# Layer 1, second head: in two quarters the normalised rows are turned by VectorE and sixteen transfers

## The reference

```python
h = jnp.maximum(_layernorm(x, axis=-1), 0.0)
x = x + _L0_gnn_ref(...)            # one normalised product with adj, W, relu
h = jnp.maximum(_layernorm(x, axis=-1), 0.0)
x = x + _L1_gnn_ref(...)            # two attention heads, below
...                                 # layer 2: one attention head; layer 3: product with adj.T
```

```python
h = x_norm @ ff0_w[i].T
s_src = h @ attn_w[i, :c]
s_dst = h @ attn_w[i, c:]
e = jax.nn.leaky_relu(s_src[:, None] + s_dst[None, :])
e = jnp.where(mask, e, jnp.float32(NEG))
atten = jax.nn.softmax(e, axis=1)
att = atten @ h + x
att = _ln(att, g2, b2)
h_next = h_next + jax.nn.elu(att @ ff1_w[i].T) / K
```

## Time and profile before

| | |
|---|---|
| median of 3 runs | 1198.27 us (1197.99 to 1199.12) |
| the profiled execution | 1198.28 us |
| its span, first to last instruction | 1196.5 us |
| mean granted clock of TensorE | 1.000 |
| PE / DVE / ACT busy | 1191.9 / 936.4 / 301.6 us |
| products of stages 1, 2 and 4 in the chain (L504) | 51% |
| products of stages 0 and 3 in the chain (L488) | 37% |

### The profile page before, as it was taken

One profiled execution on the slowest core, in us unless ns is written; L12 is line 12 of the kernel. 1 busy time (PEld: TensorE's weight loads), 2 busy tenths in 40 slices (PEclk: granted clock), 3 DMA queues, 4 the chain that ended last, 5 costly groups with the idle time before them and its releaser, 6 DMA issues.

```text
span 1196.5 us, 16807 instructions
## 1 busy us (share of the span) xinstructions
PE 1191.9 (100%) x6299; PEld 823.5 (69%) x6299; DVE 936.4 (78%) x1704; ACT 301.6 (25%) x732; POOL 10.4 (1%) x21
## 2 busy tenths in 40 slices
PE   9999999999999999999999999999999999999999
PEld 9999999965444444444544547999999974444455
DVE  5548675798878788878888796798787869887886
ACT  3312122234323232422323134541212121000000
POOL 3000000000000000000000000000000000000000
PEclk9999999999999999999999999999999999999999
DMA  9888888700111102110000000022303068999930
GB/s 318 301 270 289 299 293 302 254 23 10 45 18 36 18 35 35 53 18 18 1 18 0 18 1 19 2 86 109 141 0 141 1 258 305 313 332 319 321 85 18
DMA packets 79284, 153.18 MB, mean 128 GB/s; under 512 B 35456, under 2 KB 44016, under 8 KB 79216
## 3 DMA queue, kind: packets, MB, share of 16 engines
q1 hardware_dynamic: 53264, 145.43, 34.8%
q10 hardware_dynamic: 25456, 6.30, 2.4%
q0 software_dynamic: 496, 0.55, 0.1%
HBM read 144.33 MB, written 4.24 MB: 124 GB/s over the span
## 4 chain that ended last, share of the span: by engine, by line
PE 98%; DVE 1%; ACT 0%; issue 0%; DVEq 0%
PE acc L504 51%; PE acc L488 37%; PE acc L761 4%; PE mix L570 1%; PE mix L557 1%; PE mix L542 1%; PE turn L519 1%; PE acc L769 1%; DVE ring L1323 0%; PE turn L515 0%; PE mix L628 0%; PE mix L515 0%; PE turn L638 0%; DVE U L1454 0%; PE mix L645 0%; PE turn L633 0%
## 5 line engine op out<-in xcount | busy, mean ns | idle before, releaser
L1323 DVE SCALAR_TENSOR_TENSOR ring<-G,score,mask 128x1024 f32<-128x1024 f32 x372 | 464.7, 1279 | 62.8 <-PE acc L504 33.0
L504 PE MATMUL acc<-ring,G 128*128 128x512 f32 x1000 | 436.2, 593 | 0.2 <-DVE acc L1263 0.2
L504 PEld LDWEIGHTS acc<-ring,G 128*128 128x128 f32 x1000 | 186.6, 190 | 226.9 <-issue 209.8
L488 PE MATMUL acc<-G,ring 128*128 128x129 f32 x2240 | 254.3, 275 | 0.1
L488 PEld LDWEIGHTS acc<-G,ring 128*128 128x128 f32 x2240 | 252.1, 192 | 1.4 <-issue 1.1
L488 PE MATMUL acc<-G,mask 128*128 128x129 f32 x1648 | 186.2, 275 | 0.0
L488 PEld LDWEIGHTS acc<-G,mask 128*128 128x128 f32 x1648 | 185.0, 192 | 0.0
L504 PE MATMUL acc<-mask,G 128*128 128x512 f32 x384 | 165.8, 593 | 0.0
L1597 DVE TENSOR_TENSOR ring<-ring,mask 128x1024 f32<-128x1024 f32 x120 | 146.7, 1223 | 11.4 <-DVE ring L1597 0.9
L504 PEld LDWEIGHTS acc<-mask,G 128*128 128x128 f32 x384 | 72.6, 190 | 91.0 <-issue 89.8
L1361 DVE TENSOR_SCALAR mask<-mask 128x1024 uint8<-128x1024 f32 x103 | 68.6, 688 | 38.0 <-DMA mask<-in_adj_t 37.7
(11 more groups left out here) (210 smaller groups left out, 692.6 us busy)
## 6 DMA issues: line engine op xcount, KB each, us to landing
mask<-in_adj SPq DMA_DIRECT2D x128, 512.0 KB, 5.5
mask<-in_adj_t SPq DMA_DIRECT2D x103, 512.0 KB, 4.9
ring<-in_adj_t SPq DMA_DIRECT2D x18, 512.0 KB, 4.9
G<-given_rows SPq DMA_DIRECT2D x10, 512.0 KB, 3.9
G<-in_adj_t SPq DMA_DIRECT2D x4, 512.0 KB, 5.1
inputs<-V ACTq DMA_DIRECT2D x4, 512.0 KB, 2.7
V<-inputs SPq DMA_DIRECT2D x4, 512.0 KB, 3.9
X<-in_x SPq DMA_DIRECT2D x3, 512.0 KB, 9.9
```

The costliest lines, as they stand in the source:

```text
L488: mm = pe.matmul(acc[:, b, (s % 3) * DW:(s % 3) * DW + DW], lhs[:, s * P:(s + 1) * P], g, start=(k == 0 and s % 3 == 0), stop=(k == T - 1) ...
L504: mm = pe.matmul(acc[:, c, :], g, moving[:, c * BANK:(c + 1) * BANK], start=(k == 0), stop=(k == T - 1), skip_group_check=True)
L1323: dve.scalar_tensor_tensor(slots[k % L], late_home[h] if early and k >= EARLY else rows_home[h, q], rank[h][:, k:k + 1], span(mask, (q * T ...
```

## The change

`MOVED = 2`: for the quarters 0 and 1 of the second head, PE's `turned` is left out. In their place stand DVE's `small_turns` and `move_blocks`, eight transfers on SP's queue (behind `bring_back(0)` and `bring_back(1)`) and eight on ACT's, and ACT scales V, not `turn`. Quarters 2 and 3 keep PE's transposes. The counts of `blocks_moved` and `small_turned` for the last layer move up by two, and `move_blocks` is told by an argument which buffers it works on.

The lists of `stage2` for the quarters 1 and 2 of the loop change with it. On PE, `sums_back` stays behind tile 1, the transposes (13) go, `apply` moves from 15 to 17, the two steps of the feed stay at 27 and 28. On DVE:

| step | behind tile, before | after |
|---|---|---|
| residual, rest of it | 4, 5 | 4, 5 |
| statistics, half and rest | 8, 10 | 7, 8 |
| scales | 12 | 9 |
| small turns | - | 12 |
| own pattern, rest of it | 13, 16 | 14, 17 |
| elu, add | 19, 20 | 20, 21 |
| feed: half, rest, scales, halves | 21, 23, 25, 29 | 22, 23, 25, 29 |

```diff
--- before.py
+++ after.py
@@ -83,6 +83,7 @@
     EDGE = (2, 3, 0, 1)
     EB = len(EDGE)
     SPARE = 2
+    MOVED = 2
     WEIGHTS = 15
     WARM = 7
 
@@ -264,10 +265,10 @@
 
         flat_v = V[:, :, :].rearrange("p s d -> p (s d)")
 
-        def move_blocks(eng, q, groups):
+        def move_blocks(eng, q, groups, rows=True):
 
             eng.wait_ge(small_turned, q + 1)
-            given, taker = (U[:, 0:QC], flat_v) if q < Q else (part_turned, U[:, 0:QC])
+            given, taker = (U[:, 0:QC], flat_v) if rows else (part_turned, U[:, 0:QC])
             for i in groups:
                 for d in range(4):
                     src = given[32 * i:32 * i + 32, :].rearrange("p (s d r) -> p s d r", d=4, r=32)[:, :, d, :]
@@ -435,7 +436,9 @@
             move_blocks(sp, 3, (0, 1))
             sp.wait_ge(saved, 16 * Q)
             bring_back(0)
+            move_blocks(sp, Q, (0, 1))
             bring_back(1)
+            move_blocks(sp, Q + 1, (0, 1))
             bring_back(2)
             bring_back(3)
 
@@ -570,7 +573,7 @@
                         mm = pe.matmul(mixed[:, s * P:(s + 1) * P], U[:, s * P:(s + 1) * P], ff1T[:, h, :],
                                        start=True, stop=True, skip_group_check=True)
                     mm.then_inc(ff_done, 1)
-                return (sums_back, apply) if h == 0 else (sums_back, turned, apply)
+                return (sums_back, apply) if h == 0 or not fixed(q) or q < MOVED else (sums_back, turned, apply)
 
             def spread_top(i):
                 pe.wait_ge(top_placed, i)
@@ -712,7 +715,7 @@
                     ks = [1, 11, 12, 25, 26, 27, 29]
                     run(2, q, at(ks, steps + (lambda: spread_top(early_top[3]), lambda: spread_rows(m))))
                 else:
-                    ks = [1, 13, 15, 27, 28]
+                    ks = [1, 17, 27, 28]
                     run(2, q, at(ks, steps))
             stage2(0)
             pe.wait_ge(qv2_placed, 1)
@@ -1003,15 +1006,15 @@
                     settle()
                 normalise(of_v, lambda s: U3[:, s, 0:D], local(scale), local(shift), ACT.Identity, n_norm)
                 act.wait_ge(n_norm, j + 1)
-                if h == 0:
-                    move_blocks(act, q, (2, 3))
-                    act.wait_ge(blocks_moved, 256 * (q + 1))
+                if h == 0 or not fixed(q) or q < MOVED:
+                    move_blocks(act, j, (2, 3))
+                    act.wait_ge(blocks_moved, 256 * (j + 1))
                     for c in range(2):
                         half = slice(c * BANK, (c + 1) * BANK)
                         ins = act.activation(U[:, half], flat_v[:, half], ACT.Identity, bias=b2c, scale=g2c)
                     ins.then_inc(n_wide, 1)
                 else:
-                    widen(n_turned, q + 1, n_wide, g2c, b2c)
+                    widen(n_turned, q + 1 - MOVED, n_wide, g2c, b2c)
                 ready(ACT.Exp)
                 act.wait_ge(ff_done, j + 1)
                 act.activation(V[:, :, :], mixed3, ACT.Exp)
@@ -1097,7 +1100,7 @@
 
             def store(q):
                 wide_take(q + 4 * Q)
-                move_blocks(act, Q + q, range(4))
+                move_blocks(act, Q + MOVED + q, range(4), rows=False)
                 act.wait_ge(post_done, q + 4 * Q + 1)
                 act.dma_start(span(out.rearrange("(t p) d -> p t d", p=P), q * S, S), V[:, :, :]).then_inc(stored, 16)
             for q in range(Q - 1):
@@ -1499,7 +1502,7 @@
                 def small_turns():
                     dve.wait_ge(n_norm, j + 1)
                     dve.transpose(flat, V[:, :, :].rearrange("p s d -> p (s d)")).then_inc(small_turned, 1)
-                turns = [small_turns] if h == 0 else []
+                turns = [small_turns] if h == 0 or q < MOVED else []
                 steps = [residual, residual_rest] + statistics(lambda s: U3[:, s, 0:D], n_var) + [scal] + turns + [elu, add]
                 return steps if h == 0 else steps + [own_pattern, own_pattern_rest]
 
@@ -1542,7 +1545,7 @@
                     ks = [4, 4, 6, 8, 10, 17, 17, 12, 14, 19, 21, 24, 28, 29, 30]
                     run(2, q, at(ks, steps + early_of(3)))
                 else:
-                    ks = [4, 5, 8, 10, 12, 19, 20, 13, 16, 21, 23, 25, 29]
+                    ks = [4, 5, 7, 8, 9, 12, 20, 21, 14, 17, 22, 23, 25, 29]
                     run(2, q, at(ks, steps))
             for q in range(1, Q):
                 stage2(q)
@@ -1634,7 +1637,7 @@
 
                 def first_half():
                     st.wait()
-                    dve.wait_ge(blocks_moved, 256 * (Q + q + 1))
+                    dve.wait_ge(blocks_moved, 256 * (Q + MOVED + q + 1))
                     if q > 0:
                         dve.wait_ge(stored, q * 16)
                     st.mark(results(slice(0, HALF)))
```

## The result

Median of 20 runs 1200.07 us (1199.48 to 1200.69), against 1198.51 us (1197.92 to 1199.17, 20 runs) of the kernel before on the same chip: a ratio of 1.0014, 95% interval 1.0008 to 1.0020. The change costs 1.56 us; forecast were 1.8. The profiled execution took 1199.58 us, span 1197.8.

The account below looks back on a forecast made before the run. PE was taken to bound the kernel, busy 1191.9 of 1196.5 us. Per quarter -0.87 + 1.77 = +0.90 us, twice +1.8, on 1198.28 gave 1200.1 us; range 1196.4 to 1202.5.

Parts of the forecast that it names:

- What the removal is worth: PE in two quarters of the second head: eight transposes fewer in each, 0.87 us per quarter, 1.74 us in all.
- DVE's transpose and the wait for the rows, costed at nothing: DVE after tile 12: transpose of 1.23 us, wait for normalised rows covered by 0.3 us; a later 2.47 us wait hides both.
- The move: Transpose's end to ScalarE's scaling, 7.07 us; hidden before PE's projection after tile 17 with 2.7 us to spare.
- second rival: ScalarE's wait for the sixteen transfers ends late and PE stands before the projection: at 12 us, 1205 us; chance 0.07.
- The upper end of 9.10 us: Longest transpose-to-scaling interval in the first head, beside a 512 KB load; would leave 0.7 us to spare.
- The step that set the sign: Projection after tile 17, ELU after 20: DVE's tile 24 comes 1.46 us late, plus 0.31; PE loses 1.77 us per quarter.
- The first rival: DVE's larger lead or earlier exponentials shrink PE's pause, in the limit to nothing: 1196.5 us; chance 0.18.
- DVE behind earlier: DVE's steps drawn together make a second late tile, some 1.5 us per quarter more: 1203 us; chance 0.05.
- the clock: PE's clock falls to 1.2 GHz for the eight tiles left in a quarter, twice, 27 us: 1227 us; chance 0.02.
- the round trip exposed: Transpose, transfers and scaling all stand on the path, 7.5 us per quarter: 1213 us; chance 0.02.
- the terms given for slower: Chances of a slower result: 0.14 + 0.07 + 0.05 + 0.04, rounded to 0.28; the first as a quarter of the forecast's 0.64.
- the fourth rival: PE's clock gate closes on idling, 1.2 GHz for the rest of each of two quarters, 27 us: 1227 us; chance 0.02.

## Why the prediction was right, point by point

- *What the removal is worth.* 0.87 us per quarter was the price of the row; the changed lists without and with the exchange differ by 1201.7 - 1200.07 = 1.6 us (two groups of runs), and the kernel with the projection at 16 is 1.7 us ahead of the one before. Right.
- *DVE's transpose and the wait for the rows, costed at nothing.* The transpose started without idle time, 1.24 us, and DVE still waited 3.44 us for the exponentials afterwards. Right. The cover was as thin as said: ACT's activations started at 560.61 and took 3.19 us, so to 563.80, and the transpose started at 564.08.
- *The move.* 6.89 us, for 7.07 taken; 2.9 us to spare before the projection, for 2.7. The kernel with the projection at 15 shows that the spare time is real and ends just there, and that the second rival's mechanism exists; it isn't at work in the changed kernel. The upper end of 9.10 us was read as the price of a load beside the move. The trace of before has a second part in it: SP issued that load first, so its eight transfers started 1.32 us after the transpose's end (455.43 to 456.75), where the other quarter had 0.03 (338.13 to 338.16).

```profile
456.38 0.33 SPq L405 DMA_DIRECT2D G<-given_rows  x1
456.75 5.23 SPq L275 DMA_DIRECT2D V<-U  x8
```

- *The step that set the sign.* Tile 24 was put at 1.46 us too late and 0.31 to take it up, 1.77 us in all. It was made 590.14 - (578.40 + 10.30) = 1.44 us too late, and the loss is 1.77 by the timeline, and +0.89 and +0.90 us per quarter in the chain where +0.90 was worked out. Its cause is shown, not only argued: the places in the lists alone cost 3.3 us without any exchange, and in the changed kernel one place earlier or later for the projection takes away or adds about one PE tile per quarter.
- *The first rival, the gain stays*, needed a larger lead of DVE. Tile 16 gives that lead, and the time is that of the rival, 1196.7 for 1196.5.
- *DVE behind earlier, the clock, the round trip exposed.* None in the changed kernel: one piece of products from tile 2 to 17, a granted clock of 1.000, and no gap before the projection. Tile 9, given 0.9 us of lead, had it (made at 560.27, wanted at 549.13 + 7 x 1.717 = 561.15). The rule of the Trainium skill on transposes (VectorE: DVE Perf Modes, section Rules for kernel authors) looks right by the changed kernel's time, but for another reason than the transposes: with the projection at tile 16 the exchange against the rule is ahead.
- *What is left.* The medians differ by 1.56 us and the two quarters by 1.79. The profiled spans differ by 1.3 us, since the changed kernel's execution was 0.48 us ahead when the first changed quarter began (547.35 for 547.83). That stage is untouched; such differences are within what runs of one kernel differ by. That the forecast of 1200.1 us lies 0.03 from the median is partly luck: it was added to 1198.28, the kernel before then ran at 1198.51, and the cost came out 0.24 us smaller.
- *The chances.* A quarter of 0.64 is 0.16, not 0.14, and the terms given for slower add up to 0.30, not 0.28. Nothing else rests on them.

## What to carry to other kernels

Where one engine makes tiles just ahead of another, a step moved in the consumer's list must be counted against the producer's: write down, from the moment that releases the producer, when each of the next tiles is made and when it is wanted. Here the margin took up the first place, and the second cost 1.77 us, a whole PE tile and twice what the change had won. A round trip that is moved off the bounding engine gives two bounds, the earliest place by its own length and the latest by what waits behind it; here they left one place out of the four tried, with the producer's list kept as it was. Moving two of the producer's steps was worth 0.5 us per quarter, so both lists belong in the search.

## What the runs showed of the hardware

- *The clock.* With all transfers on one queue PE stood idle for 2.27 us in one quarter and 2.28 in the other. Ahead of both it had worked on products without a gap. Behind the first the granted clock was 0.54 over 3.5 us, close to the level of 1.2 GHz, and the projection's 16 instructions took 3.54 us; behind the second it was 1.00 and they took 2.05. The windows view of that kernel (us, busy of PE, PEld, DVE, ACT, POOL, clock):

```profile
579.50:583.00 3.50, 3.49 (x17) 3.49 (x18) 0.00 (x0) 1.47 (x2) 0.00 (x0) 0.54 0.00 0
...
647.00:650.00 3.00, 3.00 (x19) 2.23 (x18) 0.00 (x0) 2.36 (x4) 0.00 (x0) 1.00 0.00 0
```

  So the mechanism of the fourth rival exists: it followed one pause of 2.27 us and not the other of 2.28, at a far smaller price than was put on it, about 1.5 us once and not for the rest of the quarter. Its share in the median is less certain: the five executions of this kernel had mean clocks of 0.997 to 0.999, and the profiled one had 0.999, so others lost more to the clock. What decides it is not shown. That the engine's clock gate closes on idling is what the Trainium skill has (TensorE: Matmul & The Clock Gate, Part 1); the first pause agrees; behind the second, just as long, the clock stayed up. The pauses of 0.92 us in the changed kernel and of 1.04 us in the kernel with the projection at 18 left it at 1.00.
- *Issuing sets the length of many small moves.* Eight issues on each of two queues: 6.9 us from transpose to scaling; sixteen on one: 12.0 us (565.97 to 577.94). One issue took 0.68 us of its queue in the first case (5.46 / 8) and 0.66 in the second (10.55 / 16).
